# Decoder layer on one core: rows of context sums and attention constants brought to all partitions through DRAM instead of by TensorE products

## What is computed

```python
def _L0_attn_ref(x, Wqkv, bqkv, Wproj, bproj, scale):      # 1: linear attention by cumulative sums
    q, k, v = split(x @ Wqkv.T + bqkv)                     # q and k: times scale, elu, plus 1
    y = q * cumsum(k * v) / clip(sum_per_head(q * cumsum(k)), 1e-3)
    return y @ Wproj.T + bproj

def _channel_attention(qm, km, vm, scale):                 # 2: 4 heads of 128 channels, over channels
    scores = jnp.einsum('bhdn,bhen->bhde', qh, kh) * scale
    attn = jax.nn.softmax(scores, axis=-1)
    out = jnp.einsum('bhde,bhen->bhdn', attn, vh)

def _L0_xattn_ref(q, k, v, ...):                           # k and v are the context
    att_global = _channel_attention(q * wqg + bqg, k * wkg + bkg, v * wvg + bvg, scale)
    att_local  = _channel_attention(q * wql + bql, k * wkl + bkl, v * wvl + bvl, scale)
    return 2.0 * (att_global + att_local) * wp + bp

def _L0_ffn_ref(x, Wr, br, W1, b1, W2, b2):                # 3: one of 8 experts for each batch
    top1 = jnp.argmax(x.mean(axis=1) @ Wr + br, axis=-1)
    return relu(x @ W1[top1] + b1[top1]) @ W2[top1] + b2[top1]

x = _layernorm(x + _L0_attn_ref(x, ...))
x = _layernorm(x + _L0_xattn_ref(x, ctx, ctx, ...))
x = _layernorm(x + _L0_ffn_ref(x, ...))
```

## Time and profile before

| | |
|---|---|
| median of 3 runs | 2354.44 us |
| lowest, highest | 2353.5, 2355.1 us |
| span of the profiled execution, first to last instruction | 2352.2 us |
| around the span, median less span | 2.24 us |
| TensorE products busy | 2332.6 us, 99% |
| TensorE weight loads | 1927.6 us, 82% |
| VectorE | 1652.7 us, 70% |
| ScalarE | 1144.1 us, 49% |
| GpSimd | 451.6 us, 19% |
| DMA | 354.77 MB, mean 151 GB/s |

### The profile page before, as it was taken

The page is one execution under the profiler, slowest core; times in us unless marked ns, Lnnn a source line. Parts: engine busy times, 40 slices in busy tenths (PEclk is TensorE's granted clock), DMA queues, the critical chain, the costliest instruction groups (busy, mean ns, idle before and its releaser), DMA issues.

```text
span 2352.2 us, 34307 instructions
## 1 busy us (share of the span) xinstructions
PE 2332.6 (99%) x12060; PEld 1927.6 (82%) x12060; DVE 1652.7 (70%) x2863; ACT 1144.1 (49%) x1902; POOL 451.6 (19%) x395
## 2 busy tenths in 40 slices
PE   9999999999999999999999999999999999999998
PEld 7878888888888888888888888888888888888787
DVE  8886685866858668586675867758677586875643
ACT  5354445454454544545455444545454454554543
POOL 1112211121121212212122111211113111121200
PEclk9999999999999999999999999999999999999999
DMA  9255445463444634446354454544536435453332
GB/s 341 83 160 188 117 144 163 133 218 106 150 155 143 207 102 179 132 144 206 108 182 133 138 193 126 187 127 143 180 117 206 117 135 179 126 161 99 100 116 90
DMA packets 97276, 354.77 MB, mean 151 GB/s; under 512 B 11858, under 2 KB 11986, under 8 KB 86994
## 3 DMA queue, kind: packets, MB, share of 16 engines
q1 hardware_dynamic: 80210, 319.02, 38.2%
q0 software_dynamic: 16896, 33.56, 9.0%
HBM read 329.47 MB, written 23.07 MB: 150 GB/s over the span
## 4 chain that ended last, share of the span: by engine, by line
PE 92%; DVE 1%; ACT 1%; issue 1%; POOL 0%; DMA 0%; SPq 0%; POOLq 0%; DVEq 0%; ACTq 0%
PE acc L1274 29%; PE m L1049 13%; PE h_ps L1250 10%; PE h_ps L1252 10%; PE h_ps L1251 10%; PE m L1079 6%; PE m L1133 2%; PE m L1210 2%; PE m L1117 2%; PE m L1118 2%; PE m L1119 2%; PE m L1231 1%; PE m L1090 1%; PE m L1103 1%; PE acc L1290 0%
## 5 line engine op out<-in xcount | busy, mean ns | idle before, releaser
L561 ACT ACTIVATE hid<-h_ps,b 128x512 f32<-128x512 f32 x252 | 173.6, 689 | 598.2 <-PE h_ps L1252 597.5
L1049 PE MATMUL m<-xT_hi,wq 128*128 128x512 f32 x1320 | 408.2, 390 | 0.3 <-DVE xT_lo L1010 0.3
L1250 PE MATMUL h_ps<-x2T_hi,we_hi 128*128 128x512 f32 x1008 | 400.4, 397 | 2.4 <-DVE x2T_lo L905 2.4
L1274 PE MATMUL acc<-we_hi,h_hi 128*128 128x512 f32 x1008 | 400.8, 398 | 1.5 <-DVE h_lo L921 1.5
L921 DVE TENSOR_TENSOR h_lo<-hid,h_hi 128x512 fp32r<-128x512 f32 x252 | 224.3, 890 | 252.9 <-ACT h_hi L568 252.9
L1252 PE MATMUL h_ps<-x2T_hi,we_lo 128*128 128x512 f32 x1008 | 392.9, 390 | 0.0
L1274 PE MATMUL acc<-we_hi,h_lo 128*128 128x512 f32 x1008 | 392.8, 390 | 0.0
L1274 PE MATMUL acc<-we_lo,h_hi 128*128 128x512 f32 x1008 | 392.7, 390 | 0.0
L1251 PE MATMUL h_ps<-x2T_lo,we_hi 128*128 128x512 f32 x1008 | 392.4, 389 | 0.0
L911 DVE TENSOR_TENSOR we_lo<-raw,we_hi 128x1024 fp32r<-128x1024 f32 x256 | 319.9, 1250 | 31.2 <-ACT we_hi L551 31.2
L499 ACT ACTIVATE e_f<-m,sb_qkv,scale 128x512 f32<-128x512 f32 x116 | 90.5, 780 | 479.8 <-PE m L1079 477.7
(11 more groups left out here) (259 smaller groups left out, 3368.6 us busy)
## 6 DMA issues: line engine op xcount, KB each, us to landing
raw<-in_w SPq DMA_DIRECT2D x256, 512.0 KB, 4.2
wq<-wq_scratch SPq DMA_DIRECT2D x168, 512.0 KB, 3.3
x<-in_x_tok SPq DMA_DIRECT2D x16, 1024.0 KB, 5.5
x<-in_b_proj POOLq DMA_DIRECT2D x16, 1024.0 KB, 14.7
ctx_T<-in_ctxT SPq DMA_DIRECT2D x16, 1024.0 KB, 8.2
x<-in_b POOLq DMA_DIRECT2D x16, 1024.0 KB, 11.8
ctx_tok<-in_ctx_tok SPq DMA_DIRECT2D x15, 1024.0 KB, 4.7
out_dram<-x SPq DMA_DIRECT2D x15, 1024.0 KB, 4.8
```

Source lines behind the costliest of these rows:

```text
L561: act.activation(hid[:, f % 2, :], up_bank(b, f)[:, :], ACT.Relu, bias=b1[:, b % 2, f:f + 1]).then_inc(h_done, 1)
L1049: pe.matmul(bank(a, j)[:, :], w[:, s, t, :], x_hi[:, t, :], start=(t == 0 and s == 0), stop=False)
L1250: pe.matmul(ps, we_hi[:, g % NW, js], x2T_hi[:, j, :], start=(j == 0), stop=False)
L1274: last = pe.matmul(acc[t][:, :], hx[:, f % 2, ts], wx[:, g % NW, C:], start=(f == 0 and n == 0), stop=(f == FC - 1 and n == 2))
```

## The change

From batch 1 on the two rows take another way. ScalarE stores the column `c_col` (two slots after `CTX_SUM`) as a row of 512 numbers to a scratch tensor in DRAM, waits two slots later for the store, and loads the row from there into all partitions of `c_sb`. It does the same with `k_all2`: stored in slot 42, and one slot later, after waiting for the store, loaded into `const_b`. `ctx_sums` and `constants` are left to batch 0 alone, with the diagonals and copies that served them. The store's DRAM side is written as `"(h p) -> p h"`, so that each of its elements is a piece of its own.

TensorE's waits are rearranged: `x_sums` (slot 36) now waits for `scores_inner` to have read the bank, which `ctx_sums` did in slot 35, and `attend` no longer waits for the copy of the constants. VectorE's `scores_ctx` waits for the load `csum_in`, GpSimd's sum for `const_in`; the writers of `c_col` and `k_all2` wait for the stores of the batch before.

```diff
+KEEP_CSUM = plan(28, 27, 28, 29)
+LOAD_CSUM = plan(30, 29, 30, 31)
+KEEP_CONST = plan(42, 41, 45)
+LOAD_CONST = plan(43, 42, 46)
...
+    csum_dram = nc.dram_tensor("csum_scratch", [NB, C], F32, kind="Internal").ap()
+    const_dram = nc.dram_tensor("const_scratch", [NB, C], F32, kind="Internal").ap()
...
+        def by_column(row):
+            return row.rearrange("(h p) -> p h", h=XH)
...  gpsimd
-                if (c := at(i, h, WEIGH + 2)) is not None:
-                    pool.wait_ge(kall2_done, c + 1)
...
-                    diagonal(k_all2, 2 * c + 1, diag2_done)
+                if at(i, h, WEIGH + 2) == 0:
...
                 if (c := at(i, h, CONST + 1)) is not None and c > 0:
-                    pool.wait_ge(kb_done, c)
+                    pool.wait_ge(const_in, 16 * c)
...
-                if (a := at(i, h, CTX_SUM + 1)) is not None:
...
-                    diagonal(c_col, 2 * a, diag_done)
+                if at(i, h, CTX_SUM + 1) == 0:
+                    pool.wait_ge(csum_done, XH)
+                    diagonal(c_col, 0, diag_done)
...  scalar
-                if (c := at(i, h, CTX_ROW)) is not None:
-                    act.wait_ge(c_mm, c + 1)
-
-                    if (due := upto(c - 1, 12, 4)) is not None:
-                        act.wait_ge(sc_done, due)
-                    act.activation(c_sb[:, :, :], row_bank(c), ACT.Copy).then_inc(cb_done, 1)
+                if at(i, h, CTX_ROW) == 0:
+                    act.wait_ge(c_mm, 1)
+                    act.activation(c_sb[:, :, :], row_bank, ACT.Copy).then_inc(cb_done, 1)
+                if (c := at(i, h, KEEP_CSUM)) is not None and c > 0:
+                    act.wait_ge(csum_done, XH * c + XH)
+                    act.dma_start(by_column(csum_dram[c]), c_col[:, :], allow_slow_non_contiguous=True).then_inc(csum_st, 16)
+                if (c := at(i, h, LOAD_CSUM)) is not None and c > 0:
+                    act.wait_ge(csum_st, 16 * c)
+
+                    act.wait_ge(sc_done, 12 * (c - 1) + 4)
+                    act.dma_start(c_sb[:, :, :].rearrange("p h e -> p (h e)"),
+                                  csum_dram[c:c + 1, :].broadcast_to([P, C])).then_inc(csum_in, 16)
+                if (c := at(i, h, KEEP_CONST)) is not None and c > 0:
+                    act.wait_ge(kall2_done, c + 1)
+                    act.dma_start(by_column(const_dram[c]), k_all2[:, :], allow_slow_non_contiguous=True).then_inc(const_st, 16)
+                if (c := at(i, h, LOAD_CONST)) is not None and c > 0:
+                    act.wait_ge(const_st, 16 * c)
+
+                    act.wait_ge(csum_done, XH * c + XH)
+                    if c > 1:
+                        act.wait_ge(x1c_done, TT * (c - 1))
+                    act.dma_start(const_b[:, :], const_dram[c:c + 1, :].broadcast_to([P, C])).then_inc(const_in, 16)
...
-                if (c := at(i, h, CONST)) is not None and c > 0:
-                    act.wait_ge(kb_mm, c)
-
-                    act.wait_ge(csum_done, XH * c + XH)
-                    act.activation(const_b[:, :], M2[:, :], ACT.Copy).then_inc(kb_done, 1)
...  vector
-                dve.wait_ge(cb_done, c + 1)
+                if c == 0:
+                    dve.wait_ge(cb_done, 1)
+                else:
+                    dve.wait_ge(csum_in, 16 * c)
...  tensor
-            def ctx_sums(c):
-                pe.wait_ge(diag_done, c + 1)
-
-                if c > 0:
-                    pe.wait_ge(sc_done, 12 * c + 2)
+            def ctx_sums():
+                pe.wait_ge(diag_done, 1)
...  x_sums
+                pe.wait_ge(sc_done, 12 * c + 2)
                 if c == 0:
-                    pe.wait_ge(sc_done, 2)
-                pe.wait_ge(cb_done, c + 1)
+                    pe.wait_ge(cb_done, 1)
...
-            def constants(c):
-                pe.wait_ge(diag2_done, c + 1)
-
-                pe.wait_ge(aT_done, c + 1)
-                constant_rows(c, 0).then_inc(kb_mm, 1)
...  attend
-                    if c > 0:
-                        pe.wait_ge(kb_done, c)
```

More of the change, by code:

```diff
@@ L201, in build @@
         asum_done, kall_done, kall2_done, diag2_done = (sem(n) for n in ("asum_done", "kall_done", "kall2_done", "diag2_done"))
-        aT_mm, kb_mm, aT_done, kb_done, x1c_done = (sem(n) for n in ("aT_mm", "kb_mm", "aT_done", "kb_done", "x1c_done"))
+        aT_mm, aT_done, x1c_done = (sem(n) for n in ("aT_mm", "aT_done", "x1c_done"))
         out_mm, res2_done = sem("out_mm"), sem("res2_done")
@@ L225, in tr_bank @@
             return (M2, acc[2], acc[3], M0)[j] if b == 0 else (M2, M0, M1, M2)[j]
-        def row_bank(c):
-            return H_PS[:, :].rearrange("p (h e) -> p h e", h=XH) if c == 0 else by_head
+        row_bank = H_PS[:, :].rearrange("p (h e) -> p h e", h=XH)
         def ahead(a, j, t):
@@ L436, in mix @@
                         tile_sum(a, xsum_done)
-                if (c := at(i, h, WEIGH + 2)) is not None:
-                    pool.wait_ge(kall2_done, c + 1)
-                    pool.wait_ge(c_mm, c + 1)
-                    pool.wait_ge(diag_done, c + 1)
-                    diagonal(k_all2, 2 * c + 1, diag2_done)
+                if at(i, h, WEIGH + 2) == 0:
+                    pool.wait_ge(kall2_done, 1)
+                    pool.wait_ge(c_mm, 1)
+                    pool.wait_ge(diag_done, 1)
+                    diagonal(k_all2, 1, diag2_done)
                 if (z := at(i, h, FFN + 43)) is not None:
@@ L633, in mix @@
                     act.wait_ge(ctxT_in, 16 * a + 16)
-                    if (due := upto(a - 1, 1, 1)) is not None:
-                        act.wait_ge(diag_done, due)
+                    if a == 1:
+                        act.wait_ge(diag_done, 1)
+                    if (due := upto(a - 2, 16, 16)) is not None:
+                        act.wait_ge(csum_st, due)
                     if (due := upto(a - 2, TT, TT)) is not None:
@@ L1134, in gram @@
                 last.then_inc(g_mm, 1)
-            def ctx_sums(c):
-                pe.wait_ge(diag_done, c + 1)
-                if c > 0:
-                    pe.wait_ge(sc_done, 12 * c + 2)
-                pe.matmul(row_bank(c), ones_r[:, :], diag[:, 0, :, :], start=True, stop=False)
-                pe.matmul(row_bank(c), ones_r[:, :], diag[:, 1, :, :], start=False, stop=True).then_inc(c_mm, 1)
+            def ctx_sums():
+                pe.wait_ge(diag_done, 1)
+                pe.matmul(row_bank, ones_r[:, :], diag[:, 0, :, :], start=True, stop=False)
+                pe.matmul(row_bank, ones_r[:, :], diag[:, 1, :, :], start=False, stop=True).then_inc(c_mm, 1)
             def x_sums(c):
@@ L1186, in attention_T, with constant_rows @@
                 last.then_inc(aT_mm, 1)
-            def constant_rows(c, t):
-                ps = out_bank(c, t)[:, :].rearrange("p (h e) -> p h e", h=XH)
-                pe.matmul(ps, ones_r[:, :], diag[:, 0, :, :], start=(c > 0), stop=False)
+            def constant_rows(t):
+                ps = out_bank(0, t)[:, :].rearrange("p (h e) -> p h e", h=XH)
+                pe.matmul(ps, ones_r[:, :], diag[:, 0, :, :], start=False, stop=False)
                 return pe.matmul(ps, ones_r[:, :], diag[:, 1, :, :], start=False, stop=True)
-            def constants(c):
-                pe.wait_ge(diag2_done, c + 1)
-                pe.wait_ge(aT_done, c + 1)
-                constant_rows(c, 0).then_inc(kb_mm, 1)
             def attend(c, t):
@@ L1214, in attend @@
                         pe.wait_ge(diag2_done, 1)
-                    last = constant_rows(c, t)
+                    last = constant_rows(t)
                 last.then_inc(out_mm, 1)
@@ L1310, in mix @@
                     attention_T(c)
-                if (c := at(i, h, CONST)) is not None:
-                    if c > 0:
-                        constants(c)
                 for t in range(TT):
```

18 lines of the change are left out of this document (7 added, 11 removed).

## The result

The changed kernel takes 2361.13 us (median of 5 runs, 2359.38 to 2366.65) against 2354.44 before: a ratio of 1.0035, with an interval of 1.0022 to 1.0048 (the two medians alone give 1.0028). One run of the kernel before, beside the change, took 8350.22 us and is left out. The prediction had said 2339.1 us and faster. The profiled execution has a span of 2358.6 us against 2352.2, so the profile shows the same difference, +6.4 us, as the runs, +6.7.

What follows compares the result with a forecast made beforehand. TensorE, busy throughout the steady state, was taken as the bound; 13.8 us for products plus 1.5 at batch 15 made 15.3, so 2354.44 became 2339.1 us, range 2336 to 2346.

Steps and rivals of the forecast that it cites:

- The products, 13.8 us: TensorE, batches 1 to 15: four 128x512 products removed per batch, 0.92 us each batch, 13.8 us for the kernel.
- Batch 15, 1.5 us: Batch 15: without the diagonal, VectorE's `h_lo` ends earlier and TensorE's 1.55 us wait goes; 1.5 us taken, bounds nothing and 2.5.
- What is L1?: Time from issue to landing of the constants' store in slot 43's wait: 5.5 us taken, 3.3 to 7.6 held likely.
- The context sums have much room: ScalarE's sums transfer: 12.8 us for the store to land, rows first read 28 us after the load; cost nothing.
- LOAD_CONST ... have little: Constants' transfer in the steady batch: little cover, but store 5.5 us and load 4 both fit, costing TensorE nothing.
- L1 of 9.3: Steady batch: TensorE loses time once the constants' store takes 9.3 us to land; the batch's gain is gone at about 10.2.
- L1 + L2 of 16: Steady batch: constants' store and load together may take 14.6 us before residual 0, or 16 with 1.4 us of slack.
- Every further microsecond would be one: Constants' transfer: if its cover were gone, each further microsecond would cost one microsecond in each of 15 batches.
- The one that I gave 0.08: Rival at `LOAD_CONST`: store lands late, ScalarE blocks TensorE's work; 2365 us just past the point, up to 2474; chance 0.08.

Runs made afterwards that it cites:

- the kernel with 16-byte pieces: The changed kernel with each DRAM row laid out by partition, stores of 128 pieces of 16 bytes, readers using a strided view: 2341.36 us, ratio 0.9952 to the kernel before.

## Why the prediction was wrong, step by step

**The products, 13.8 us: right.** Batches that nothing disturbs are shorter by 0.9 us, and the kernel with 16-byte pieces has a span of 2339.1 us against 2336.9 worked out. Its `gram` starts at 149.37, 279.89 and 2144.26 in batches 1, 2 and 15, which places the 2.2 us that are missing: 0.5 lies ahead of the `gram` of batch 1, as in the two runs that send nothing through DRAM there (0.4 and 0.5); the 13 stretches from batch 2 to 15 give 0.83 each instead of 0.92, 1.1 together; and what follows gives 0.96 beyond its products instead of 1.5.

**Batch 15, 1.5 us: right in mechanism.** The wait for `h_lo` goes with the constants' diagonal: it is there in the kernel before and in the two of the experiments that keep that diagonal in batch 15, and in none that lacks it. VectorE's operation falls from 2.38 to 0.68 us, as the Trainium skill's rule has it (SBUF — State Buffer, "Who interferes with whom"). With 16-byte pieces TensorE's waits behind that `gram` are 1.36 us shorter than before and the end is 0.96 beyond the products, inside my bounds of nothing and 2.5. But in the change a new wait of 3.00 us took the place of the one of 1.55, which I had looked for only in the steady batch.

**"What is L1?": the step that failed.** I took 5.5 us, and 7.6 as the far end. It is 9.0 and 10.1 in the change. The row that I was nearest to by size, `b<-in_b` at 3.3 us, was of another kind in two ways: it was a load, and its pieces were 64 bytes. Loads and wider pieces don't show the cost: the load of 128 neighbours of 4 bytes took 2.0 us, the store 6.7. No store of small pieces was in the trace, so no row bounded this from above but the 18.3 us, and between 3.3 and 18.3 I narrowed the range by a sum of packets that held for reads. The width that I gave the forecast should have been that of the bounds.

The Trainium skill (DMA: Bandwidth & Descriptors, "Rules for kernel authors") had warned of the strided last dimension, and this trace agrees that each element is a piece of its own: ScalarE's queue has 20160 packets, and 8640 with 16-byte pieces, the difference being 30 x 384. My estimate from that page was 7.4 us, worked out from figures that it gives for DMAs issued by GpSimd, and loads at that; the same store, issued by ScalarE, takes 9.8 alone. By its rule on pieces under 512 bytes ("Specifications") those of 16 are read and modified too, and they land in 1.4 us alone. The measurement decides: what cost the time here was mostly neighbours.

**"The context sums have much room": wrong.** I measured the room to the reader of the rows, 28 us, and the 12.8 us between store and load in the steady batch. In batch 2 ScalarE comes to its wait 4.1 us behind the store, which lands after 9.3, and `x2T_hi` is what stands behind the wait. Store and wait must be priced in every batch in which other work stands between them.

**"LOAD_CONST ... have little": right place, wrong batch.** The two limits that I gave for the steady batch, L1 of 9.3 and L1 + L2 of 16, stand against 10.1 and 15.9: past the first, just within the second, and by my numbers the change would have lost 0.8 us a batch. Batch 9 lost nothing, since ScalarE issued the store 1.5 us earlier than I had it: not when it comes free of `r_f`, but together with `e_f`, at 1342.68. The two batches that crossed the edge in earnest had less cover. In batch 1, TensorE asks for `aT` 8.6 us behind the store's issue (202.39 to 211.0), in batch 9 13.9 us behind it (1342.68 to 1356.55). For residual 0 it asks in batch 1 16.7 us behind the issue, 12.4 without the first wait of 2.55 and the 1.7 of slower products after it, and in batch 9 20.2. A cover read from one batch was carried to fifteen.

**The price of a wait: too low.** "Every further microsecond would be one" holds for the wait only. Each idle time of 2.4 to 3.0 us was followed by a stretch at 1.2 GHz that cost 1.6 to 2.1 us more, so 7.72 us of waits between the `gram` of batch 1 and that of batch 2 cost 13.1. The shorter ones, 1.26 us in batch 2, 0.99 in batch 7 and 0.97 in batch 15, were followed by a granted clock of 1.00; the stretches of batches 2 and 7 lost 0.4 and 0.3 us beyond them.

**The rivals.** The one that I gave 0.08, the store late and ScalarE in front of TensorE's work, is nearest: it had the right transfer, the right direction and, just past its point, 2365 us. But it is not the blocked ScalarE alone that decides: with the wait moved out of its way TensorE stood for residual 0 instead, and the time was 2367.76 us. It is two late ends of the constants' transfers and one of the sums', in three batches, rather than one in fifteen.

## What to carry to other kernels

Keep a small row in DRAM in the order in which the partitions hold it, and let the reader turn it: the same 2 KB went from 9.0 us to 1.4 (the sums) and from 10.1 to 3.5 (the constants), for a strided view that costs GpSimd and VectorE some time and TensorE none. Price a new wait in the first and the last stage as well as in the steady one, and by what is queued behind it, not by who reads its data. Where TensorE had never been idle, a wait of 2.4 to 3.0 us cost its own length and some 0.6 to 0.9 of it again in clock, one of 1.0 to 1.3 us its own length and 0.3 to 0.4 us.

## What the runs showed of the hardware

- Stores of 4-byte pieces side by side in DRAM are slow even with nothing else under way: 128 of them 6.7 us, 128 that are 64 bytes apart 1.4 us, 512 of them 9.8 us.
- They slow the other queue's packets too. The weights' queue moves the same 80210 packets in every kernel; their time is 38.2% of 16 engines' span before, 41.9% in the change and 38.3% with 16-byte pieces, 0.179, 0.197 and 0.179 us for each. With one of the two rows alone it is 39.9 and 39.7%.
- ScalarE's queue issued the store while activations ahead of it in the program were still to be done: at 1342.68, with the start of `e_f` and 0.68 us before that of `r_f` (1343.36). So a DMA can overtake work of its own engine on which it doesn't wait, which the description ahead of the prediction rules out. The issue takes 0.33 to 0.36 us with 128 pieces and 0.38 to 0.42 with 512.
- TensorE's granted clock stayed at 1.00 behind waits of 0.97, 0.99 and 1.26 us and fell behind those of 2.36, 2.55, 2.81 and 3.00 us, where products of 128x512 started 0.43 us apart instead of 0.23.
